# VectorE's order in the first product of a sparse feed-forward layer: an operation moved behind the second low part of w1, dot products regrouped

## The chip, the cores and the metric

The kernel runs on one NeuronCore of a Trainium2 chip (trn2). The metric is the device time of one execution in microseconds (us), as the median of several runs; lower is better.

## What is computed

A cross-attention layer is followed by a feed-forward layer in which each token uses only 56 of 3584 hidden rows. Both are residual. The change concerns the feed-forward layer alone:

```python
inter = xf @ c1_w.T @ c2_w.T                     # (1600, 3584), rank 16
blk = inter.reshape(B * T, n_blocks, SPARSITY)   # 56 blocks of 64
idx = jnp.argmax(blk, axis=-1) + jnp.arange(0, INTER, SPARSITY)
w1_g = w1[idx]
w2_g = w2t[idx]
h = jax.nn.relu(jnp.einsum('bkm,bm->bk', w1_g, xf))
out = jnp.einsum('bk,bkm->bm', h, w2_g)
```

There are 16 x 100 = 1600 tokens of 1024 features, all in float32. The attention ahead of it projects queries, keys and values, attends and projects back (`x1 = x + attention`).

## The kernel before

The stages follow each other, each in a block of its own with a barrier at its end: keys and values, queries, attention, the output projection, a normalisation, the gate's weights, then `hidden_layer` (the first product of the sparse layer, where the change is) and `project_down` (the second).

**Most tokens go the dense way.** For 1344 tokens `hidden_layer` computes the whole of `w1 @ x1t` and multiplies it by a mask of ones and zeros that holds the argmax. A float32 product is made of three products of high and low parts (`product`, 8 chunks x 3 = 24 matmuls of 128x336). w1 has 28 blocks of 128 rows, taken two at a time: 14 bodies (`i`), each of two halves (`p` = 0, 1), and block `j = 2i + p`. A half has four tiles of 336 tokens (`t` = 0 to 3), and so four calls of `sums(j, p, t)` on TensorE.

**256 tokens go the gathered way.** For them GpSimd gathers the chosen rows of w1 from DRAM into a ring of four buffers (`hid_ring`), and VectorE takes the dot product of each with its token (`dot(k)`): six per body from the second body on, 78 in all. A gather is issued when the dot product four places before it is done (`dotted`).

What each engine does in one half, in program order:

- TensorE: `sums` 0; `turn_w` (four transposes, the first half of the next block of w1, into PSUM bank `turn` 0); `gates` (the gate values of four token tiles, or one); `sums` 1; `turn_w` for the second half, into `turn` bank 1; `sums` 2; then the wait `pe.wait_ge(low, 2 * j + 4)`, for both low parts of the next block; `turn_mask` (11 and 2 transposes of the mask, into the same two banks, which is why they must be free); `gates` again; `sums` 3. A `sums` of tile `t` waits for `evacuate` of tile `t` of the half before.
- ScalarE: `high_part` rounds each half of the transposed w1 into `hid_w` (L1749), and `mask_part` copies the transposed mask into `hid_mask_t` (L1758).
- VectorE, the engine whose order is changed: `low_part` 0 and 1 (what the rounding left over, L1779); `pick`, which finds the argmax of a group of gate values in five operations: max (L1793), equality with it (L1795), multiplication by keys (L1797), max (L1801) and the mask itself (L1803); `indices` (once a body, L1809); `evacuate` 0 to 3 (relu and mask from PSUM to `h`, L1827); the `dot`s (L1546); and once a body `clip` (L1551). `evacuate` 0 waits for the transposed mask.
- SyncE loads blocks of w1 and stores `h` to `h_scratch`, after `evacuate` 3 of each half.

The first body is a special case: its first half makes all masks of the first pair, its second half (`late`) makes an extra one, and it has no dot products. The last body makes no masks.

In the trace `hid_raw` and `c_raw` are the loaded blocks of w1 (and `c_raw` also `h`), `turn` is the PSUM tile of transposes, `hid_acc` the PSUM tile of the sums, `w_l_raw` and `w_w_raw` the operands of `project_down`.

Of the kernel before, what the change touches and what calls it, by code (L numbers as in the profile page):

```python
# [1557 lines left out]
def hidden_layer(nc, sem, w1, x1t, c2s, zs, h_dram, ident, ident_bf, sparsity, stored, sparse, spare):  # L1558
# [11 lines left out]
    per = 2 * P // sparsity  # L1570

    picks = [(a, min(4, tt - a)) for a in range(0, tt, 4)]
    NP = len(picks)
# [11 lines left out]
    with ExitStack() as mem:  # L1585
# [31 lines left out]
        @block.sync  # L1617
        def _(sp):
            def load(j, p):
                sp.dma_start(raw[p][:, :], w1_v[bass.ds(j, 1)].rearrange("a p n -> (a p) n")).then_inc(landed[p], 16)  # L1620

            def store(j, p):
                sp.wait_ge(h_out, tiles * (j + 2))
                sp.dma_start(h_dram[bass.ds(j, 1)].rearrange("a p n -> (a p) n"), h[p][:, :]).then_inc(stored[p], 16)

            load(0, 0)
            load(1, 1)
            with sp.Fori(0, pairs - 1) as i:
                for p in range(2):

                    sp.wait_ge(turned, 2 * (2 * i + p + 1))
                    load(2 * i + p + 2, p)
                    store(2 * i + p, p)
            store(blocks - 2, 0)
            store(blocks - 1, 1)
# [139 lines left out]
        @block.vector  # L1775
        def _(dve):
            def low_part(j, p, s):
                dve.wait_ge(high, 2 * j + s + 1)
                dve.tensor_tensor(w[p][:, 1, 4 * s:4 * s + 4, :], turn[:, s, :].rearrange("q (c n) -> q c n", c=4),  # L1779
                                  w[p][:, 0, 4 * s:4 * s + 4, :].bitcast(F32), ALU.subtract).then_inc(low, 1)  # L1780

            def spread(ap, g):
                return ap.rearrange("q (a c) -> q a c", c=1).to_broadcast([P, g, sparsity])

            def pick(i, m, k):

                a, n = picks[k]
                g = n * per
                at = slice(a * per, a * per + g)
                done = NP * i + k  # L1790
                values = gate[:, :, :].rearrange("q a (b c) -> q (a b) c", c=sparsity)[:, :g, :]
                dve.wait_ge(gated, done + 1)
                dve.tensor_reduce(top[:, at], values, AX.X, ALU.max).then_inc(step, 1)  # L1793
                dve.wait_ge(step, 3 * done + 1)
                dve.tensor_tensor(equal[:, at, :], values, spread(top[:, at], g), ALU.is_equal).then_inc(compared, 1)  # L1795
                dve.wait_ge(compared, done + 2)
                dve.tensor_tensor(equal[:, at, :], equal[:, at, :],  # L1797
                                  key_bf[:, :].rearrange("q (a c) -> q a c", a=1).to_broadcast([P, g, sparsity]),
                                  ALU.mult).then_inc(step, 1)
                dve.wait_ge(step, 3 * done + 2)  # L1800
                dve.tensor_reduce(lead[:, at], equal[:, at, :], AX.X, ALU.max).then_inc(step, 1)  # L1801
                dve.wait_ge(step, 3 * done + 3)
                dve.tensor_tensor(mask[m][:, at, :], equal[:, at, :], spread(lead[:, at], g),  # L1803
                                  ALU.is_equal).then_inc(masked, 1)

            def indices(i):

                at = slice(i * per, (i + 1) * per)
                dve.tensor_tensor(sparse.idx[:, :, at],  # L1809
                                  base[:, at].rearrange("q (a c) -> q a c", a=1).to_broadcast([P, sparse.S, per]),  # L1810
                                  lead[:, :sparse.S * per].rearrange("q (a c) -> q a c", a=sparse.S),
                                  ALU.subtract).then_inc(idx_made, 1)

            def dot(k):
                kind, s, g = sparse.hidden[k]
                dve.wait_ge(gathered[k % slots], 16 * (k // slots + 1))
                sparse.dot(dve, s, g, ring[k % slots]).then_inc(dotted, 1)

            def evacuate(i, p, t):
                j = 2 * i + p  # L1820
                dve.wait_ge(summed, tiles * (j + 1) + t + 1)
                if t == 0:
                    dve.wait_ge(mask_out, 2 * j + 4)

                    dve.wait_ge(stored[p], 16 * (i + 1))
                at = slice(t * width, (t + 1) * width)
                dve.scalar_tensor_tensor(out=h[p][:, at], in0=acc[:, t, :width], scalar=0.0, in1=mask_t[:, at],  # L1827
                                         op0=ALU.max, op1=ALU.mult).then_inc(h_out, 1)

            def body(i, m, more, first):  # L1830
                for p in range(2):
                    j = 2 * i + p
                    early = first and p == 0
                    late = first and p == 1
                    dots = [] if first else [sparse.PER_PAIR * (i - 1) + sparse.PER_PAIR // 2 * p + n
                                             for n in range(sparse.PER_PAIR // 2)]
                    if early:
                        for k in range(NP):
                            pick(0, 0, k)
                            if k == 0:  # L1840
                                indices(0)
                    if late:
                        pick(1, 1 - m, 1)
                    if more or p == 0:
                        low_part(j + 1, 1 - p, 0)
                    if more and not early:
                        pick(i + 1, 1 - m, 2 * p)
                        if p == 0:
                            indices(i + 1)
                    if more or p == 0:  # L1850
                        low_part(j + 1, 1 - p, 1)
                    evacuate(i, p, 0)
                    for k in dots[:1]:
                        dot(k)
                    evacuate(i, p, 1)
                    if more:
                        pick(i + 1, 1 - m, 0 if early else 2 * p + 1)
                        if early:
                            indices(i + 1)
                    for k in dots[1:2]:  # L1860
                        dot(k)
                    evacuate(i, p, 2)
                    for k in dots[2:]:
                        dot(k)
                    evacuate(i, p, 3)
                if not first:
                    dve.wait_ge(dotted, sparse.PER_PAIR * i)
                    sparse.clip(dve, range(sparse.PER_PAIR * (i - 1), sparse.PER_PAIR * i)).then_inc(clipped, 1)

            dve.wait_ge(made, 2)  # L1870
            dve.wait_ge(base_made, 1)
            low_part(0, 0, 0)
            low_part(0, 0, 1)
            for i in range(pairs):
                body(i, i % 2, i + 1 < pairs, i == 0)
# [550 lines left out]
```

## Time and profile before

| | before |
|---|---|
| median of 3 runs | 3725.41 us (3724.01 to 3728.13) |
| the profiled execution | 3725.45 us, of which the span is 3723.7 us |
| granted TensorE clock, mean of the span | 0.973 of full speed |
| TensorE busy | 3479.5 us, 93% of the span |
| VectorE busy | 2323.2 us, 62% |
| ScalarE, GpSimd busy | 1415.3 us, 38%; 837.3 us, 22% |

The span is the time between the first and the last instruction that the profiler recorded; the execution's own time is 1.75 us longer. The granted clock is told as a share of 2.4 GHz. Busy shares are averages over all stages; what a change in one stage is worth has to be read from that stage, which here lasts from 2669 to 3208 us of the span.

### The profile page before, as it was taken

Reading aid. Unit: us, or ns where it says so; the run is one execution under the profiler, and the core shown is the slowest. Engines: PE = TensorE matmul, PEld = TensorE weight load, DVE = VectorE, ACT = ScalarE, POOL = GpSimd, SP = SyncE. Lnnn points to the kernel's source line nnn. Section 1 sums busy time; section 2 is a strip of 40 time slices with the busy share of each in tenths; the row PEclk is TensorE's granted clock in tenths of the full one; section 3 lists DMA queues with packets and bytes.
Section 4 is the critical chain, followed back from the end, with each engine's and each line's share of the span. In section 5 each row is a group of like instructions: output and inputs, shape, how many; then the busy total and the mean of one; then the engine's idle time right before and its main releaser. Section 6 shows DMA issues by size and latency. Waiting matters only on the chain. (4 is left out here: it accounts for less than half of the span.)

```text
span 3723.7 us, 52261 instructions
## 1 busy us (share of the span) xinstructions
PE 3479.5 (93%) x18370; PEld 3066.9 (82%) x18370; DVE 2323.2 (62%) x3935; ACT 1415.3 (38%) x2648; POOL 837.3 (22%) x1100
## 2 busy tenths in 40 slices
PE   6999999899999999999998999999799999699899
PEld 5888888799998888888887787787689999677676
DVE  5555575877665777777775333332578888566765
ACT  4333343444333777777775222221411111221321
POOL 0000000000002667666662100000011111233231
PEclk8999999899999999999999999999899999899999
DMA  3333333454444333333334545543334443698986
GB/s 124 100 105 97 99 98 90 115 134 115 121 121 124 103 108 90 105 104 108 105 86 145 144 118 154 154 119 93 110 116 150 143 154 137 254 287 277 302 285 199
DMA packets 525094, 520.73 MB, mean 140 GB/s; under 512 B 177668, under 2 KB 413188, under 8 KB 524884
## 3 DMA queue, kind: packets, MB, share of 16 engines
q1 hardware_dynamic: 489220, 391.06, 35.5%
q0 software_dynamic: 34608, 124.90, 10.1%
q8 instruction: 117, 1.92, 0.2%
q10 hardware_dynamic: 1056, 2.10, 0.2%
q14 instruction: 93, 0.76, 0.1%
HBM read 402.95 MB, written 115.02 MB: 139 GB/s over the span
## 5 line engine op out<-in xcount | busy, mean ns | idle before, releaser
L2083 PE MATMUL wo_acc<-wo_w,wo_l 128*128 128x512 f32 (+1 forms) x2496 | 573.7, 392 | 21.9 <-DVE wo_l L2033 21.8
L427 PE MATMUL kv_bank<-kv_wo,kv_so 128*128 128x512 f32 x2436 | 575.7, 396 | 15.8 <-DVE kv_wo L519 10.6
L2083 PEld LDWEIGHTS wo_acc<-wo_w,wo_l 128*128 128x128 f32 (+1 forms) x2496 | 460.2, 185 | 135.2 <-DVE wo_w L2057 24.7
L427 PEld LDWEIGHTS kv_bank<-kv_wo,kv_so 128*128 128x128 f32 x2436 | 458.7, 190 | 110.6 <-issue 16.7
L815 PE MATMUL pr_bank<-pr_xo,pr_wp 128*128 128x400 f32 x2688 | 500.6, 348 | 27.5 <-ACT pr_s L882 11.9
L815 PEld LDWEIGHTS pr_bank<-pr_xo,pr_wp 128*128 128x128 f32 x2688 | 495.4, 191 | 30.4 <-DVE pr_wp L899 22.6
L2312 PE MATMUL w_acc<-w_w,w_l 128*128 128x512 f32 (+1 forms) x1848 | 451.5, 404 | 60.9 <-DVE w_l L2287 60.0
L2312 PEld LDWEIGHTS w_acc<-w_w,w_l 128*128 128x128 f32 (+1 forms) x1848 | 344.8, 189 | 167.3 <-DVE w_l L2287 36.9
L26 PE MATMUL hid_acc<-x1t,hid_w 128*128 128x336 f32 x2688 | 442.6, 323 | 1.4 <-DVE c_raw L1827 0.9
L26 PEld LDWEIGHTS hid_acc<-x1t,hid_w 128*128 128x128 f32 x2688 | 426.4, 194 | 2.1 <-issue 1.1
L1311 PE MATMUL outs<-pt,v 128*128 128x384 f32 (+3 forms) x1536 | 347.3, 348 | 27.9 <-issue 14.0
L1409 DVE TENSOR_TENSOR pt<-turned,pt 128x512 fp32r<-128x512 f32 x384 | 264.1, 688 | 155.6 <-ACT pt L1361 152.6
L2033 DVE TENSOR_TENSOR wo_l<-wo_l_raw,wo_l 128x512 fp32r<-128x512 f32 (+1 forms) x208 | 139.4, 672 | 335.2 <-ACT wo_l L2006 335.1
L26 PE MATMUL scores<-kt,q_parts 128*128 128x462 f32 x1152 | 337.8, 402 | 1.2 <-ACT probs L1367 1.2
L1311 PEld LDWEIGHTS outs<-pt,v 128*128 128x128 f32 (+1 forms) x1536 | 277.4, 188 | 66.2 <-issue 30.4
L1239 POOL TENSOR_SCALAR probs<-probs,inverse 128x461 f32<-128x461 f32 x400 | 261.6, 654 | 249.9 <-DVE inverse L1405 249.7
L1361 ACT ACTIVATE pt<-turned 128x512 fp32r<-128x512 f32 x384 | 229.3, 597 | 168.5 <-PE turned L1292 165.2
L2006 ACT ACTIVATE wo_l<-wo_l_raw 128x512 fp32r<-128x512 f32 (+1 forms) x208 | 127.6, 615 | 397.7 <-PE wo_acc L2083 378.3
L1367 ACT ACTIVATE probs<-scores,negmax 128x461 f32<-128x461 f32 x400 | 257.6, 644 | 35.6 <-DVE negmax L1398 34.3
L1398 DVE TENSOR_REDUCE negmax<-scores 128x1 f32<-128x461 f32 x400 | 251.2, 628 | 23.8 <-PE scores L1276 23.2
L1292 PE MATMUL turned<-ident,probs 128*128 128x128 f32 x1600 | 240.7, 273 | 1.2 <-POOL probs L1239 1.2
L2244 ACT ACTIVATE w_l<-w_l_raw 128x512 fp32r<-128x512 f32 (+1 forms) x154 | 93.9, 611 | 335.5 <-DMA w_l_raw<-h_scratch 269.7
(185 smaller groups left out, 4182.3 us busy)
## 6 DMA issues: line engine op xcount, KB each, us to landing
wo_l_raw<-o_scratch SPq DMA_DIRECT2D x192, 256.0 KB, 2.9
w_l_raw<-h_scratch SPq DMA_DIRECT2D x140, 256.0 KB, 4.6
pair_raw<-in_L_xattn_Wq_dram SPq DMA_DIRECT2D x64, 512.0 KB, 5.6
q_scratch<-pr_out SPq DMA_DIRECT2D x128, 200.0 KB, 2.4
o_scratch<-o_stage SPq DMA_DIRECT2D x64, 400.0 KB, 3.5
q_raw<-q_scratch SPq DMA_DIRECT2D x64, 384.0 KB, 3.2
stage<-in_ctx_dram SPq DMA_DIRECT2D x45, 512.0 KB, 3.9
h_scratch<-c_raw SPq DMA_DIRECT2D x28, 672.0 KB, 5.5
```

The lines of the kernel that those rows point to most:

```text
L26: last = pe.matmul(out, left(a, c), right(b, c), start=(c == 0 and (a, b) == PAIRS[0]), stop=(c == chunks - 1 and (a, b) == PAIRS[-1]))
L427: last = pe.matmul(bank[:, BANK[i], :], so[:, i, a, c, :], wo[:, i, e, c, :], start=(not opened and c == 0 and (a, e) == PAIRS[0]), stop=( ...
L815: last = pe.matmul(bank[:, BANK[i], :width], wo[:, i, a, c, :], xo[:, i, e, c, :], start=(not opened and c == 0 and (a, e) == PAIRS[0]), s ...
L1239: pool.tensor_scalar(probs[:, I % RB, :kv], probs[:, I % RB, :kv], inverse[:, I % RB:I % RB + 1], 1.0, ALU.mult, ALU.mult).then_inc(scaled, 1)
L1292: last = pe.transpose(turned[:n, j % TB, k, :], probs[:, j % RB, at:at + n], ident[:, :])
L1311: last = pe.matmul(outs[:, h, :hi - lo], v[b % 2][:n, a, k, g * P:(g + 1) * P], pt[:n, e, k, lo:hi], start=(x == 0), stop=(x == NC * len(P ...
L1361: act.activation(pt_of(j, 0), turned[:, j % TB, :, :], ACT.Copy).then_inc(pt_high, 1)
L1367: act.activation(probs[:, I % RB, :kv], scores[:, I % SB, :kv], ACT.Exp, bias=negmax[:, I % RB:I % RB + 1], accum_out=total[:, I % RB:I % ...
L1398: dve.tensor_reduce(negmax[:, I % RB:I % RB + 1], scores[:, I % SB, :kv], AX.X, ALU.max, negate=True).then_inc(s_max, 1)
L1409: dve.tensor_tensor(pt_of(j, 1), turned[:, j % TB, :, :], pt_of(j, 0).bitcast(F32), ALU.subtract).then_inc(pt_low, 1)
L2083: last = pe.matmul(acc[p][:rows, :], l[j % 2][:, a, k, :rows], w[:, c, m * per + k, :], start=(m == 0 and k == 0 and (a, c) == PAIRS[0]), ...
L2312: last = pe.matmul(acc[n % 2][:heights[t], :], l[u % 2][:, a, k, :heights[t]], w[:, c, m * per + k, :], start=(m == 0 and k == 0 and (a, c ...
```

## The change

The mask operation is split off from `pick` into a function of its own, `mark`. In a half of a steady body the second `low_part` now stands between the two, so that it comes ahead of the mask operation. The dot products of a body, three in each half before, are now two in the first half and four in the second; the first two of a half stand in front of `evacuate` 0, where before only single ones stood between the evacuations. `evacuate` 0, 1 and 2 now follow each other, and the second `pick` of a half comes behind `evacuate` 2. No operation is added or taken away.

```diff
                 dve.tensor_reduce(lead[:, at], equal[:, at, :], AX.X, ALU.max).then_inc(step, 1)
+
+            def mark(i, m, k):
+
+                a, n = picks[k]
+                g = n * per
+                at = slice(a * per, a * per + g)
+                done = NP * i + k
                 dve.wait_ge(step, 3 * done + 3)
                 dve.tensor_tensor(mask[m][:, at, :], equal[:, at, :], spread(lead[:, at], g),
                                   ALU.is_equal).then_inc(masked, 1)
...
-                    dots = [] if first else [sparse.PER_PAIR * (i - 1) + sparse.PER_PAIR // 2 * p + n
-                                             for n in range(sparse.PER_PAIR // 2)]
+                    at = sparse.PER_PAIR * (i - 1)
+                    dots = [] if first else list(range(at, at + 2) if p == 0 else range(at + 2, at + sparse.PER_PAIR))
                     if early:
                         for k in range(NP):
                             pick(0, 0, k)
+                            mark(0, 0, k)
                             if k == 0:
                                 indices(0)
                     if late:
                         pick(1, 1 - m, 1)
+                        mark(1, 1 - m, 1)
                     if more or p == 0:
                         low_part(j + 1, 1 - p, 0)
                     if more and not early:
                         pick(i + 1, 1 - m, 2 * p)
+                    if more or p == 0:
+                        low_part(j + 1, 1 - p, 1)
+                    if more and not early:
+                        mark(i + 1, 1 - m, 2 * p)
                         if p == 0:
                             indices(i + 1)
-                    if more or p == 0:
-                        low_part(j + 1, 1 - p, 1)
+                    for k in dots[:2]:
+                        dot(k)
                     evacuate(i, p, 0)
-                    for k in dots[:1]:
-                        dot(k)
                     evacuate(i, p, 1)
+                    evacuate(i, p, 2)
                     if more:
                         pick(i + 1, 1 - m, 0 if early else 2 * p + 1)
+                        mark(i + 1, 1 - m, 0 if early else 2 * p + 1)
                         if early:
                             indices(i + 1)
-                    for k in dots[1:2]:
-                        dot(k)
-                    evacuate(i, p, 2)
                     for k in dots[2:]:
                         dot(k)
                     evacuate(i, p, 3)
```

What stands in VectorE's program, in a steady body, from `evacuate` 0 of the first half to the first low part of the second half (`hid_w0`), in the kernel before. The instruction with L1546 is a dot product; the one after it, which writes `value` alone, reads its sum out.

```order
L1827 SCALAR_TENSOR_TENSOR c2_raw<-hid_acc,hid_mask_t 128x336 [waits h_stored0,mask_out,h_summed]
L1546 ISA hid_ring0,value<-hid_ring0,keep0 128x1024 [waits row_gathered0]
L1546 ISA value 128x1
L1827 SCALAR_TENSOR_TENSOR c2_raw<-hid_acc,hid_mask_t 128x336 [waits h_summed]
L1793 TENSOR_REDUCE hid_top<-gate 128x16 [waits gated]
...
L1803 TENSOR_TENSOR hid_mask0<-hid_equal,hid_lead 128x1024 [waits mask_step]
L1546 ISA hid_ring1,value<-hid_ring1,keep1 128x1024 [waits row_gathered1]
L1546 ISA value 128x1
L1827 SCALAR_TENSOR_TENSOR c2_raw<-hid_acc,hid_mask_t 128x336 [waits h_summed]
L1546 ISA hid_ring2,value<-hid_ring2,keep0 128x1024 [waits row_gathered2]
L1546 ISA value 128x1
L1827 SCALAR_TENSOR_TENSOR c2_raw<-hid_acc,hid_mask_t 128x336 [waits h_summed]
L1779 TENSOR_TENSOR hid_w0<-turn,hid_w0 128x512 [waits w1_high]
```

The same place in the changed kernel, from two dot products on:

```order
L1546 ISA hid_ring0,value<-hid_ring0,keep0 128x1024 [waits row_gathered0]
L1546 ISA value 128x1
L1546 ISA hid_ring1,value<-hid_ring1,keep1 128x1024 [waits row_gathered1]
L1546 ISA value 128x1
L1834 SCALAR_TENSOR_TENSOR c2_raw<-hid_acc,hid_mask_t 128x336 [waits h_stored0,mask_out,h_summed]
L1834 SCALAR_TENSOR_TENSOR c2_raw<-hid_acc,hid_mask_t 128x336 [waits h_summed] x2
L1793 TENSOR_REDUCE hid_top<-gate 128x16 [waits gated]
...
L1810 TENSOR_TENSOR hid_mask0<-hid_equal,hid_lead 128x1024 [waits mask_step]
L1834 SCALAR_TENSOR_TENSOR c2_raw<-hid_acc,hid_mask_t 128x336 [waits h_summed]
L1779 TENSOR_TENSOR hid_w0<-turn,hid_w0 128x512 [waits w1_high]
```

Between the wait for the mask and the low part `hid_w0` there were three dot products; now there is none. One of them has gone to the second half, two stand ahead of the wait.

The second place is the start of the second half of a body on VectorE. Before:

```order
L1779 TENSOR_TENSOR hid_w0<-turn,hid_w0 128x512 [waits w1_high]
L1793 TENSOR_REDUCE hid_top<-gate 128x16 [waits gated]
L1795 TENSOR_TENSOR hid_equal<-gate,hid_top 128x1024 [waits mask_step]
L1797 TENSOR_TENSOR hid_equal<-hid_equal,hid_key_bf 128x1024 [waits compared]
L1801 TENSOR_REDUCE hid_lead<-hid_equal 128x16 [waits mask_step]
L1803 TENSOR_TENSOR hid_mask0<-hid_equal,hid_lead 128x1024 [waits mask_step]
L1779 TENSOR_TENSOR hid_w0<-turn,hid_w0 128x512 [waits w1_high]
L1827 SCALAR_TENSOR_TENSOR c2_raw<-hid_acc,hid_mask_t 128x336 [waits h_stored1,mask_out,h_summed]
```

Now, with the same five rows ahead of them:

```order
L1801 TENSOR_REDUCE hid_lead<-hid_equal 128x16 [waits mask_step]
L1779 TENSOR_TENSOR hid_w0<-turn,hid_w0 128x512 [waits w1_high]
L1810 TENSOR_TENSOR hid_mask0<-hid_equal,hid_lead 128x1024 [waits mask_step]
L1546 ISA hid_ring2,value<-hid_ring2,keep0 128x1024 [waits row_gathered2]
L1546 ISA value 128x1
L1546 ISA hid_ring3,value<-hid_ring3,keep1 128x1024 [waits row_gathered3]
L1546 ISA value 128x1
L1834 SCALAR_TENSOR_TENSOR c2_raw<-hid_acc,hid_mask_t 128x336 [waits h_stored1,mask_out,h_summed]
```

The second low part has moved ahead of one mask operation, and two dot products stand between the mask operation and `evacuate` 0.

## Rows read from the trace of the kernel before

**Rows 1.** The page: TensorE's and VectorE's busy time.

```profile
PE 3479.5 (93%) x18370; PEld 3066.9 (82%) x18370; DVE 2323.2 (62%) x3935; ACT 1415.3 (38%) x2648; POOL 837.3 (22%) x1100
```

**Rows 2.** Waits, 2669 to 3212 us: total us, times, longest.

```profile
DVE c_raw L1827 <- issue: 73.2, 27, 10.5
...
PE turn L1691 <- DVE hid_w L1779: 30.8, 14, 3.9
```

**Rows 3.** Timeline of TensorE, one body: start, us, what, count, [idle before <- releaser].

```profile
3144.41 3.93 PE L26 MATMUL hid_acc<-x1t,hid_w 128*128 128x336 f32 x24
3148.19 0.87 PE L1691 MATMUL turn<-ident_bf,hid_mask 128*128 128x128 bf16 x11
...
3149.56 7.60 PE L26 MATMUL hid_acc<-x1t,hid_w 128*128 128x336 f32 x48
3157.00 0.60 PE L1668 MATMUL turn<-ident,c_raw 128*128 128x128 f32 x4
...
3161.60 0.60 PE L1668 MATMUL turn<-ident,c_raw 128*128 128x128 f32 x4
3161.96 3.94 PE L26 MATMUL hid_acc<-x1t,hid_w 128*128 128x336 f32 x24
3167.99 0.86 PE L1691 MATMUL turn<-ident_bf,hid_mask 128*128 128x128 bf16 x11 [2.10 <-DVE hid_w L1779]
```

**Rows 4.** Timeline of VectorE, the same body.

```profile
3150.29 0.51 DVE L1827 SCALAR_TENSOR_TENSOR c_raw<-hid_acc,hid_mask_t 128x336 f32<-128x336 f32 x1 [2.57 <-issue]
3150.71 1.21 DVE L1546 CUSTOM_DVE_ANT_0 hid_ring<-hid_ring,keep 128x1024 f32<-128x1024 f32 x1
...
3151.85 0.50 DVE L1827 SCALAR_TENSOR_TENSOR c_raw<-hid_acc,hid_mask_t 128x336 f32<-128x336 f32 x1
3152.27 1.22 DVE L1793 TENSOR_REDUCE hid_top<-gate 128x16 f32<-128x1024 f32 x1
...
3156.76 1.22 DVE L1803 TENSOR_TENSOR hid_mask<-hid_equal,hid_lead 128x1024 bf16<-128x1024 bf16 x1
...
3161.02 0.68 DVE L1779 TENSOR_TENSOR hid_w<-turn,hid_w 128x512 fp32r<-128x512 f32 x1
3161.62 1.22 DVE L1793 TENSOR_REDUCE hid_top<-gate 128x16 f32<-128x1024 f32 x1
...
3166.11 1.22 DVE L1803 TENSOR_TENSOR hid_mask<-hid_equal,hid_lead 128x1024 bf16<-128x1024 bf16 x1
3167.25 0.68 DVE L1779 TENSOR_TENSOR hid_w<-turn,hid_w 128x512 fp32r<-128x512 f32 x1
```

**Rows 5.** Timeline of ScalarE, the same body: the first high part.

```profile
3157.63 0.60 ACT L1749 ACTIVATE hid_w<-turn 128x512 fp32r<-128x512 f32 x1 [7.43 <-PE turn L1668]
```

**Rows 6.** Timeline of TensorE: mask transposes of bodies 0, 1 and 5, second halves.

```profile
2714.22 1.41 PE L1691 MATMUL turn<-ident_bf,hid_mask 128*128 128x128 bf16 x11 [3.92 <-DVE hid_w L1779]
...
2753.89 0.90 PE L1691 MATMUL turn<-ident_bf,hid_mask 128*128 128x128 bf16 x11 [2.13 <-DVE hid_w L1779]
...
2904.77 1.41 PE L1691 MATMUL turn<-ident_bf,hid_mask 128*128 128x128 bf16 x11 [2.10 <-DVE hid_w L1779]
```

**Rows 7.** Stretches: length, busy us (PE, PEld, DVE, ACT, POOL), granted clock, DMA share, GB/s.

```profile
60.00:620.00 560.00, 560.00 (x2684) 467.85 (x2683) 321.53 (x562) 214.37 (x322) 6.61 (x8) 1.00 0.32 98
...
2904.77:2941.80 37.03, 36.33 (x243) 35.46 (x243) 30.06 (x45) 5.09 (x8) 6.93 (x6) 0.95 0.40 136
...
3131.00:3167.99 36.99, 34.89 (x243) 34.14 (x244) 31.40 (x46) 5.09 (x8) 6.93 (x6) 1.00 0.42 149
```

**Rows 8.** Timeline of the stage's last microseconds.

```profile
3202.49 0.51 DVE L1827 SCALAR_TENSOR_TENSOR c_raw<-hid_acc,hid_mask_t 128x336 f32<-128x336 f32 x1 [10.51 <-issue]
...
3207.17 0.50 DVE L1827 SCALAR_TENSOR_TENSOR c_raw<-hid_acc,hid_mask_t 128x336 f32<-128x336 f32 x1
...
3207.70 0.34 SPq L1624 DMA_DIRECT2D h_scratch<-c_raw  x1
```

**Rows 9.** The gathers' landing, 2740 to 3200 us.

```profile
DMA to landing us min/median/max: 3.8/6.5/9.0
```

## The prediction

> **What bounds the kernel now.** I read the page first: TensorE is busy 93% of the span, VectorE 62% [rows 1]. So VectorE can only matter where TensorE waits for it. The list of waits for the stretch of this stage shows one such place of size: the transposes of the mask waited 30.8 us in 14 waits for a low part of w1, the longest 3.9 us [rows 2]. The other direction is in the same list: `evacuate` stood idle 73.2 us in 27 times, put down to "issue" [rows 2]; its place in the program is behind the transposes and ScalarE's copy of the mask. So VectorE is late in one place and has idle time in another, once in each half.
>
> The two timelines of one body show where. TensorE starts the last `sums` ahead of the mask at 3144.41 and the mask's transposes at 3148.19, 3.78 us later, in the first half. In the second half it takes from 3161.96 to 3167.99, which is 6.03 us, with 2.10 us of idle time ahead of the transposes [rows 3]. The reader is to take the difference, 6.03 - 3.78 = 2.25 us, as the price of the wait, since it also holds the tail of a matmul whose end is only modelled. VectorE in that time [rows 4] starts the half's first low part at 3161.02, though ScalarE had the high part ready at 3157.63 + 0.60 = 3158.23 [rows 5]; it then runs five operations of `pick` and starts the second low part at 3167.25. It is 2.8 us late when the half begins.
>
> Third, the granted clock. The start of the mask's transposes in the second half repeats from 2714.22 (body 0) to 3167.99 (body 12) [rows 3, 6]: 12 periods in 453.77 us, 37.81 us each. A clean one is 36.99 us at a granted clock of 1.00 [rows 7]. The excess is 453.77 - 12 x 36.99 = 9.9 us. It comes in lumps: 2.7 us in the first period (2714.22 to 2753.89, 39.67 us), behind the longest wait, and 7.2 us in the other eleven. Where a lump begins, the eleven transposes behind the wait take 1.41 us in place of 0.86 [rows 3, 6], and the stretch that starts there has a clock of 0.95 [rows 7]: a short time at the lower of the two levels, 1.2 GHz, just behind a wait.
>
> **The change part by part.** No operation is added or removed, on any engine, and no DMA. All counts stay; only when things happen moves. I lay out the second half anew with the pitches (start to start) of the rows, and the first half's transposes at 3148.19 as before.
>
> *Dot products out of the way.* `evacuate` 0 starts at 3150.29, fixed by the mask [rows 4]. Then `evacuate` 1 and 2 at 0.42 us (3151.85 to 3152.27) each, so `pick` starts at 3151.13 + 0.42 = 3151.55; its first four operations take 4.49 us (3152.27 to 3156.76) and the mask operation 1.14 us (3166.11 to 3167.25): 3157.18; `evacuate` 3: 3157.60 [rows 4]. The first low part was at 3161.02 and could now start at 3157.60, but the high part is there only at 3158.23 [rows 5]. The three dot products that left this path gave 3 x 1.14 us (3150.71 to 3151.85) = 3.42 us, of which 2.79 us can be used.
>
> *Mask operation behind the low part.* From 3158.23: low part 0.60 us, four operations 4.49 us, so the second low part starts at 3163.32 (its high part is ready at 3161.60 + 0.63 + 0.60 = 3162.83) and ends 0.68 us later, at 3164.00 [rows 3 to 5]. TensorE would want it at 3161.96 + 3.78 = 3165.74 [rows 3]. It is 1.7 us early, and the whole 2.25 us of the wait go. Body 1 to 12: **12 x 2.25 = 27.0 us**.
>
> *What takes the dot products' place.* Behind the second low part come the mask operation (from 3163.92 to 3165.06) and two dot products. No row shows two in a row. Bounds: 1.14 us each, as ahead of an evacuation, or the full 1.22 + 0.08 us of operation and read-out, 1.30 us. They end at 3167.34 to 3167.66; the mask for `evacuate` 0 comes 2.10 us (3150.29 - 3148.19) behind the transposes, at 3167.84 [rows 3, 4]. They fit in idle time by 0.2 to 0.5 us, so they cost nothing; without that cover, `evacuate` 0 still has to be done only when TensorE starts `sums` 0, at 1.37 + 7.44 / 2 = 5.1 us behind the transposes (3148.19 to 3149.56, and half of 3149.56 to 3157.00), against 2.10 + 0.51 us [rows 3, 4]: 2.5 us to spare. The first half is alike. Its low part moved 1.14 us ahead where TensorE did not wait for it, worth nothing. SyncE's store follows `evacuate` 3, which in both halves comes no later than before; the next load of w1 behind it in the queue moves with it. GpSimd's gathers start when a dot product ends. The tightest pair of ring buffers is freed at 3167.3 and wanted by the next body's first half, whose `evacuate` 0 is at 3165.74 + 17.19 + 2.10 = 3185.03 (17.19 = 36.99 - 19.80, a clean body less 3148.19 to 3167.99 [rows 3, 7]), less two dot products: 15 us, against 9.0 us for the slowest landing [rows 9].
>
> A rule of the skill speaks against counting pitches like this. The evacuation's row says 0.50 us, but the next operation starts 0.42 us after it [rows 4]. The Trainium skill (VectorE: DVE Perf Modes, section "The DRAIN you can't avoid") holds that the next operation does not start until the pipe is empty, chained or not. By the rule three evacuations and two dot products cost 3 x 0.51 + 2 x 1.30 = 4.1 us instead of 3.5 us. The first low part would still be on time, and the sum would lose 0.5 us at the stage's tail.
>
> *The clock.* With no wait in front of them the lumps of bodies 2 to 12 should not start: **7.2 us**. The evidence is that a stretch of 560 us in which TensorE was never idle has a clock of 1.00 throughout [rows 7].
>
> *Body 0.* Its second half waits 3.92 us [rows 6]; only the mask operation moves there, 1.14 us. A shorter wait remains (2.8 us), between the 2.1 us of the others and 3.9 us. The lump of 2.7 us behind it is bounded by its whole size and by nothing; I take 0.6 us of it, since the wait that is left is longer than waits that were followed by one. **1.7 us**.
>
> *Tail.* In the last half the six operations from `evacuate` 0 (3202.49) to the start of `evacuate` 3 (3207.17) take 4.68 us [rows 8]; now one of three dot products stands ahead, so 3 x 0.42 + 2 x 1.14 (or 1.30) = 3.54 to 3.86 us. The store of `h` at 3207.70 follows directly and the next stage waits for it [rows 8]. **1.0 us**.
>
> **Sum.** 27.0 + 7.2 + 1.7 + 1.0 = 36.9 us. The profiled execution took 3725.45 us (span 3723.7 us), the median of three runs is 3725.41 us, so the two are the same here. 3725.4 - 36.9 = **3688.5 us**.
>
> **Rivals.**
> *The clock lumps stay* though the waits go, as something that comes with time and not with waits. For it: of twelve waits of about 2.1 us only some were followed by one. Against it: each begins at a wait, and none in the 560 us stretch. Then 27.0 + 1.1 + 1.0 = 29.1 us: 3696.3 us. Chance 0.10.
> *A shorter wait takes its place*, for instance for a low part that is still late because evacuations and dot products overlap less than I assume, or because TensorE, never stopping, wants it earlier. The margin of 1.7 us speaks against it. If 1 us per body stays, with half the lumps, 12 + 3.6 us are lost: 3704 us. Chance 0.05.
> *Only the mask operation's place matters*: the first low part does not start earlier, because something else than dot products holds it. Then 13 x 1.14 + 1.0 = 15.8 us: 3709.6 us. The idle-free row of VectorE up to 3161.02 [rows 4] speaks against it. Chance 0.03.
> *Slower: gathered rows come late.* Dot products now stand ahead of `evacuate` 0, which TensorE's next `sums` waits for, and in VectorE's queue everything else stands behind them, low parts too. If rows took longer than 15 + 2.5 us, every further microsecond would stop TensorE. To end 0.2% above before, it must eat 36.9 + 7.5 = 44.4 us in 12 bodies, 3.7 us each: rows that take 21 us from their buffer's release, against 9.0 us at most from issue [rows 9]. At 22 us it gives 3725.4 + 10 = 3736 us. Chance 0.03.
>
> **How the numbers follow.** My forecast holds 0.79. The time is that of the likeliest case. Its own bounds are 3686 (all of body 0's lump, full tail) to 3691 us (neither, and the drain rule); a few us more because runs of one kernel spread, the three shown by 4 us. With the clock rival inside, the range is 3685 to 3697 us and leaves out about 0.12. About 0.2% (7.5 us) is what a measurement of this kernel can tell from no change. All cases but the last are faster by more: 0.95; some 0.02 for a gain that is used up elsewhere; slower 0.03.
>
> **What the profile of the changed kernel would show.** The wait of the mask's transposes for a low part falls from 30.8 us in 14 waits to about 4.5 us in 2, both in body 0 (30.8 - 12 x 2.10 - 1.14). The mask's transposes of second halves repeat at 34.7 us (36.99 - 2.25). The granted clock is 1.00 in every body from the third on. The first low part of a second half has idle time of about 0.6 us ahead, put down to ScalarE, and the second none. Two dot products in a row are 1.14 to 1.30 us apart, which settles the drain rule. `evacuate` keeps an idle time, now under 1 us. The prediction is wrong if TensorE's list of waits shows a new one (for `hid_acc`, or for the gate's equality), if VectorE waits for gathered rows, or if lumps of clock stay in bodies that have no wait.

## The result and the profile after

The changed kernel takes 3689.74 us (median of four runs, 3684.86 to 3693.77) against 3724.71 us (four runs, 3720.31 to 3728.13) for the kernel before: a ratio of 0.9906, with a 95% interval of 0.9889 to 0.9923. That is 35.0 us less, where 36.9 us were forecast; 3689.74 us stands against a predicted 3688.5 us. The profiled execution took 3689.50 us, with a span of 3687.8 us.

The page's busy times and the list of waits of the changed kernel, from 2669 to 3175 us; a wait row has the total in us, the number of times and the longest.

```profile
PE 3460.4 (94%) x18370; PEld 3052.4 (83%) x18370; DVE 2321.1 (63%) x3935; ACT 1415.4 (38%) x2648; POOL 829.7 (22%) x1100
```

```profile
DVE hid_w L1779 <- ACT hid_w L1749: 38.4, 27, 6.1
DVE c_raw L1834 <- issue: 26.2, 28, 10.2
...
PE turn L1691 <- DVE hid_w L1779: 4.3, 2, 2.7
...
PE hid_acc L26 <- DVE c_raw L1834: 0.9, 1, 0.9
```

VectorE does the same work as before in 2321 us (2323 us in [rows 1]). What has changed is where its idle time lies. TensorE's wait for the low part has gone from 30.8 us in 14 waits [rows 2] to 4.3 us in 2. VectorE now waits more for ScalarE's high parts (38.4 us in 27 times, 23.2 us in 15 before), and less for the mask (26.2 us against 73.2 us).

Timeline of TensorE in one steady body of the changed kernel:

```profile
3013.81 0.87 PE L1691 MATMUL turn<-ident_bf,hid_mask 128*128 128x128 bf16 x11
...
3027.58 3.93 PE L26 MATMUL hid_acc<-x1t,hid_w 128*128 128x336 f32 x24
3031.35 0.87 PE L1691 MATMUL turn<-ident_bf,hid_mask 128*128 128x128 bf16 x11
...
3066.09 0.87 PE L1691 MATMUL turn<-ident_bf,hid_mask 128*128 128x128 bf16 x11
```

From the start of the last sums ahead of the mask to the start of its transposes it is now 3031.35 - 3027.58 = 3.77 us, as long as in the first half; in the kernel before it was 6.03 us in this place [rows 3]. A body lasts 3066.09 - 3031.35 = 34.74 us. Timeline of VectorE in the same body:

```profile
3013.12 1.22 DVE L1546 CUSTOM_DVE_ANT_0 hid_ring<-hid_ring,keep 128x1024 f32<-128x1024 f32 x1
3014.26 0.08 DVE L1546 DVE_READ_ACCUMULATOR2_ANT value<- 128x1 f32 x1
3014.26 1.22 DVE L1546 CUSTOM_DVE_ANT_0 hid_ring<-hid_ring,keep 128x1024 f32<-128x1024 f32 x1
3015.41 0.08 DVE L1546 DVE_READ_ACCUMULATOR2_ANT value<- 128x1 f32 x1
3015.91 1.34 DVE L1834 SCALAR_TENSOR_TENSOR c_raw<-hid_acc,hid_mask_t 128x336 f32<-128x336 f32 x3 [0.42 <-issue]
3017.16 1.22 DVE L1793 TENSOR_REDUCE hid_top<-gate 128x16 f32<-128x1024 f32 x1
...
3023.88 0.69 DVE L1779 TENSOR_TENSOR hid_w<-turn,hid_w 128x512 fp32r<-128x512 f32 x1 [0.59 <-ACT hid_w L1749]
...
3028.86 0.68 DVE L1779 TENSOR_TENSOR hid_w<-turn,hid_w 128x512 fp32r<-128x512 f32 x1
3029.45 1.22 DVE L1810 TENSOR_TENSOR hid_mask<-hid_equal,hid_lead 128x1024 bf16<-128x1024 bf16 x1
```

The first low part of the second half starts 3023.88 - 3013.81 = 10.07 us behind the first half's transposes, held by ScalarE and no longer by dot products; before it was 12.83 us (3161.02 - 3148.19 [rows 3, 4]). The second starts at 15.05 us and ends 1.8 us before TensorE wants it. The two dot products of a half end 0.4 to 0.5 us before the mask is there. Three evacuations go from 3015.91 to 3017.16 in pitch, 0.42 us each, and a dot product follows another after 1.14 us.

The stretches of the changed kernel: length, busy us of PE, PEld, DVE, ACT, POOL, granted clock, DMA share, GB/s.

```profile
2717.31:2753.49 36.18, 36.18 (x244) 35.56 (x244) 28.48 (x39) 5.09 (x8) 2.11 (x2) 0.95 0.29 97
2753.49:2788.23 34.74, 34.74 (x246) 34.15 (x244) 31.30 (x47) 5.09 (x8) 6.34 (x6) 1.00 0.47 161
...
2822.97:3135.55 312.58, 312.58 (x2188) 307.25 (x2188) 281.57 (x415) 45.83 (x72) 57.02 (x54) 1.00 0.46 161
```

From 2753.49 to 3135.55 us, from the mask's transposes in the second half of body 1 to those of body 12, TensorE is busy all the time and its clock is at 2.4 GHz throughout. Behind the second half of body 0 one lump of lower clock is left, behind the wait of 2.66 us: 36.18 - 34.74 = 1.4 us.

For the experiments I use a length that the rest of the kernel does not touch, called the stretch below: from the first transposes of the mask in the stage to the start of the last evacuation. The timelines have its start in the kernel before,

```profile
2692.12 0.86 PE L1691 MATMUL turn<-ident_bf,hid_mask 128*128 128x128 bf16 x11 [1.64 <-DVE hid_w L1779]
```

and, in the changed kernel, its start, the gates product and the first sums of body 0's second half behind it, and its end:

```profile
2696.50 0.86 PE L1691 MATMUL turn<-ident_bf,hid_mask 128*128 128x128 bf16 x11 [1.63 <-DVE hid_w L1779]
2697.29 1.10 PE L1679 MATMUL gate<-c2s,zs 80*128 80x256 f32 x4
2699.25 6.20 PE L26 MATMUL hid_acc<-x1t,hid_w 128*128 128x336 f32 x24 [0.86 <-DVE c_raw L1834]
```

```profile
3173.59 0.50 DVE L1834 SCALAR_TENSOR_TENSOR c_raw<-hid_acc,hid_mask_t 128x336 f32<-128x336 f32 x1
```

It was 3207.17 [rows 8] - 2692.12 = 515.05 us before and is 3173.59 - 2696.50 = 477.09 us now, 37.96 us less. Outside it the two profiled executions differ in stages that the change does not touch: the stretch started 4.38 us later and what follows it took 2.37 us less, which gives 35.95 us, the difference of the two executions (3725.45 - 3689.50). In the traces of all kernels here the program ahead of this point is the same, and the stretch starts anywhere between 2690.82 and 2698.82 us.

### The profile page after: what moved, and what is told of

Its sections match the earlier page's. It is cut to its first block and busy times, and to the rows that moved or that the text cites. A ratio compares the mean times of both kernels' runs of the same rounds, so it can differ in the third digit from the quotient of the medians.

```text
span 3687.8 us, 52261 instructions
## 1 busy us (share of the span) xinstructions
PE 3460.4 (94%) x18370; PEld 3052.4 (83%) x18370; DVE 2321.1 (63%) x3935; ACT 1415.4 (38%) x2648; POOL 829.7 (22%) x1100
```

## The experiments

All are built on the changed kernel and were run beside the kernel before. Four ran on one chip (kernel before 3721.76 us) and four on another (3728.55 us), neither time beside the runs of the result, so kernels of different occasions are compared by their ratios and by their stretches.

**Only the mask operation moved.** Dot products and evacuations stand as before.

```diff
-                    at = sparse.PER_PAIR * (i - 1)
-                    dots = [] if first else list(range(at, at + 2) if p == 0 else range(at + 2, at + sparse.PER_PAIR))
+                    dots = [] if first else [sparse.PER_PAIR * (i - 1) + sparse.PER_PAIR // 2 * p + n
+                                             for n in range(sparse.PER_PAIR // 2)]
...
-                    for k in dots[:2]:
-                        dot(k)
                     evacuate(i, p, 0)
+                    for k in dots[:1]:
+                        dot(k)
                     evacuate(i, p, 1)
-                    evacuate(i, p, 2)
                     if more:
                         pick(i + 1, 1 - m, 0 if early else 2 * p + 1)
                         mark(i + 1, 1 - m, 0 if early else 2 * p + 1)
...
+                    for k in dots[1:2]:
+                        dot(k)
+                    evacuate(i, p, 2)
```

Expected: 

> Only the mask operation is moved behind the second low part; dot products and evacuations stand as in the kernel before. Path theory (TensorE's wait is the time by which the second low part is late, and each operation moved off the way to it counts with its pitch): the wait of bodies 1 to 12 falls from 2.25 us by 1.14 us to 1.1 us each (about 0.96 us in the trace's idle column), that of body 0 from 3.9 to 2.7 us. The stage gets shorter by 13 x 1.14 = 14.8 us, and by up to 9.9 us more if the shorter waits are no longer followed by lumps of lower clock: 3700 to 3710 us. Rival (the mask operation's place alone made the gain): no wait in bodies 1 to 12, 3690 to 3692 us. Rival (lumps of lower clock come with time, not with waits): as the path theory, with about as many lumps as before, so at 3709 us whatever the waits are.

Measured: 3699.09 us, ratio 0.9936 (0.9922 to 0.9949). That is 0.9 us under the expected range, on a chip where the kernel before took 3.0 us less than in the result. The list of waits of this kernel, 2660 to 3212 us, and its stretches:

```profile
PE turn L1691 <- DVE hid_w L1779: 14.3, 14, 2.7
```

```profile
2714.86:2752.04 37.18, 36.34 (x244) 35.57 (x244) 27.78 (x40) 5.09 (x8) 3.46 (x3) 0.95 0.26 83
2752.04:3143.00 390.96, 382.61 (x2667) 374.64 (x2668) 341.24 (x504) 56.02 (x88) 76.16 (x66) 1.00 0.44 155
```

Of the 14.3 us, 4.3 us are the two waits of body 0, as in the changed kernel, so 10 us are left for twelve bodies: 0.8 us each in the idle column. A body is 35.73 us (3109.31 - 2752.04 over ten), 1.0 us above 34.74 us where 1.1 us was expected. Behind these short waits the clock stayed at 1.00. So, made alone, the mask's move is worth 36.99 - 35.73 = 1.26 us in each of twelve bodies, 15 us, beside it the 7.2 us of lumps in these bodies, and the same 2.5 us in body 0 as in the changed kernel. The stretch is 3184.20 - 2693.99 = 490.21 us, 24.8 us less than before. The path theory holds, and the rival that the mask operation's place alone made the gain falls: this kernel keeps a wait in each body, which costs 1.0 us. The rival on the clock expected 3709 us, with as many lumps as before, and falls too.

**Only the dot products regrouped.** The mask operation stands ahead of the second low part, as before.

```diff
-                    if more or p == 0:
-                        low_part(j + 1, 1 - p, 1)
                     if more and not early:
                         mark(i + 1, 1 - m, 2 * p)
                         if p == 0:
                             indices(i + 1)
+                    if more or p == 0:
+                        low_part(j + 1, 1 - p, 1)
```

Expected: 

> Only the dot products and evacuations are regrouped; the mask operation stays ahead of the second low part. Path theory: the first low part starts when its high part is there, 2.8 us earlier than before; the second then starts 0.60 + 4.49 + 1.14 us later and ends 0.6 us before TensorE wants it. No wait in bodies 1 to 12 and no lumps there, body 0 as in the kernel before (wait 3.9 us and its lump, together 2.5 us more than in the changed kernel): 3692 us. Rival (both edits are needed, because the second low part is 1.1 us late without the mask's move): 12 x 1.1 us and some lumps more than the changed kernel, 3703 to 3712 us. Rival (dot products were in idle time anyway and their place is worth nothing): 3725 us.

Measured: 3686.26 us, ratio 0.9905 (0.9890 to 0.9921), which can't be told from the changed kernel by time. The waits:

```profile
PE turn L1691 <- DVE hid_w L1779: 5.6, 2, 3.9
```

There is no wait in bodies 1 to 12. In one of them VectorE's second low part starts at 3029.81 and so ends at 3030.49 us, 0.6 us before TensorE starts the mask's transposes at 3031.05 us. The stretch is 3173.28 - 2693.57 = 479.71 us, 2.6 us longer than in the changed kernel (expected: 2.5 us), all of it in body 0, whose wait is 3.9 us again. So in the steady bodies the regrouping alone takes away the whole wait; beside it, the mask's move only widens the margin there, and what it adds in the changed kernel is in body 0. The rival that both edits are needed falls.

**The work put back on the path.** In the second half of bodies 1 to 12 the mask operation and the two dot products stand ahead of the second low part.

```diff
+                    behind = p == 1 and more and not first
+                    if behind:
+                        mark(i + 1, 1 - m, 2 * p)
+                        for k in dots[:2]:
+                            dot(k)
                     if more or p == 0:
                         low_part(j + 1, 1 - p, 1)
-                    if more and not early:
+                    if more and not early and not behind:
...
-                    for k in dots[:2]:
+                    for k in [] if behind else dots[:2]:
```

Expected: 

> The changed kernel, but in the second half of bodies 1 to 12 the mask operation and the two dot products stand ahead of the second low part instead of behind it. VectorE does the same work in the same half, in another order. Path theory: the second low part starts 1.14 + 2 x 1.14 us later, uses up the margin of 1.7 us and is 1.7 us late: 12 x 1.7 = 20 us more than the changed kernel, and 0 to 9 us for lumps of lower clock that come back behind the waits: 3710 to 3719 us. Rival (what helped is that VectorE's load is spread better over the halves, not the place of single operations): 3690 us. Rival on the clock (lumps come with time): one lump as in the changed kernel, 3710 us.

Measured: 3716.98 us, ratio 0.9992 (0.9982 to 1.0002): nearly all of the gain is gone. The waits, TensorE's timeline around one wait that was followed by a lump, and two bodies, the first without and the second with one:

```profile
PE turn L1691 <- DVE hid_w L1779: 24.0, 14, 2.7
```

```profile
2791.83 0.86 PE L1691 MATMUL turn<-ident_bf,hid_mask 128*128 128x128 bf16 x11 [1.64 <-DVE hid_w L1779]
...
2792.84 9.08 PE L26 MATMUL hid_acc<-x1t,hid_w 128*128 128x336 f32 x48
...
2829.82 0.86 PE L1691 MATMUL turn<-ident_bf,hid_mask 128*128 128x128 bf16 x11 [1.64 <-DVE hid_w L1779]
...
2830.84 7.59 PE L26 MATMUL hid_acc<-x1t,hid_w 128*128 128x336 f32 x48
```

```profile
2755.30:2791.83 36.53, 34.89 (x244) 34.14 (x244) 31.38 (x46) 5.10 (x8) 6.34 (x7) 1.00 0.44 153
2791.83:2829.82 37.99, 36.35 (x244) 35.61 (x244) 31.38 (x46) 5.10 (x8) 6.33 (x7) 0.96 0.43 147
```

A body without a lump is 36.53 us, 1.79 us above the changed kernel's (expected: 1.7 us), with the same 31.4 us of VectorE's work in it. After some of the waits of 1.64 us the 48 matmuls that follow take 9.08 us instead of 7.59 us. The stretch is 3202.66 - 2696.53 = 506.13 us, 29.0 us longer than in the changed kernel: 12 x 1.79 = 21.5 us for the waits and 7.5 us, five lumps of 1.5 us, for the clock. How the load is spread over the halves is the same as in the changed kernel, so the rival that this made the gain falls. The rival on the clock falls too: it expected no lumps beyond that of the changed kernel. Why five of the twelve waits, all of 1.64 us, were followed by a lump and the others not stays open.

**Body 0 in another order.** Its second half has both low parts ahead of the second search, the evacuations behind it, and two mask operations behind these.

```diff
                     if late:
                         pick(1, 1 - m, 1)
-                        mark(1, 1 - m, 1)
+                        low_part(j + 1, 1 - p, 0)
+                        low_part(j + 1, 1 - p, 1)
+                        pick(i + 1, 1 - m, 2)
+                        evacuate(i, p, 0)
+                        evacuate(i, p, 1)
+                        evacuate(i, p, 2)
+                        mark(1, 1 - m, 1)
+                        mark(i + 1, 1 - m, 2)
+                        pick(i + 1, 1 - m, 3)
+                        mark(i + 1, 1 - m, 3)
+                        evacuate(i, p, 3)
+                        continue
```

Expected: 

> The changed kernel with another order in the second half of body 0 alone: both low parts stand ahead of the second search for the maximum, and two mask operations behind the evacuations. Path theory: both low parts are there when ScalarE has the high parts, some 2 us before TensorE wants them, so the wait of 2.66 us goes, and with it the lump of 1.4 us behind it: 4.1 us less than the changed kernel, 3685.6 us. Rival (the lump stays, since the clock is low early in the stage for another reason): 2.7 us less, 3687 us. Rival (evacuation 0, behind the search, is now late and stops the next sums of TensorE): a wait of hid_acc for evacuation takes the place, 0 to 2 us less or more.

Measured: 3682.63 us, ratio 0.9886 (0.9871 to 0.9901). TensorE in body 0 of this kernel:

```profile
2698.82 0.86 PE L1691 MATMUL turn<-ident_bf,hid_mask 128*128 128x128 bf16 x11 [1.64 <-DVE hid_w L1779]
2699.62 0.74 PE L1679 MATMUL gate<-c2s,zs 80*128 80x256 f32 x4
2701.57 3.93 PE L26 MATMUL hid_acc<-x1t,hid_w 128*128 128x336 f32 x24 [1.22 <-DVE c_raw L1834]
...
2710.91 0.71 PE L1679 MATMUL gate<-c2s,zs 80*128 80x256 f32 x4 [0.82 <-DVE hid_equal L1795]
...
2715.59 0.86 PE L1691 MATMUL turn<-ident_bf,hid_mask 128*128 128x128 bf16 x11
```

The wait ahead of the last row is gone and so is the lump behind it. The stretch is 3170.49 - 2698.82 = 471.67 us, 5.4 us less than in the changed kernel where 4.1 us was expected. The difference is the clock once more: the first sums of the second half took 3.93 us here, and 6.20 us at the lower clock in the changed kernel, while a gates product now waits 0.82 us for an equality that VectorE has not done. No evacuation became late. This part is not shown to be the edit's: the gates product ahead of these sums already took 0.74 us in place of 1.10 us, before TensorE reaches anything that the edit moved, and the same order of body 0 had 5.48 us for the same sums in the experiment "Body 0 and four dot products together". What the path theory named, the wait and the lump behind it, accounts for 2.8 + 1.4 = 4.2 us. What put the clock higher in those first sums was not tested.

The other four ran together, with the changed kernel itself beside the three others.

**The changed kernel again.** Expected: 

> The changed kernel once more, on the same chip and beside the same runs as the three kernels below. Every theory expects what was measured of it: about 3689 us, between 0.989 and 0.992 of the kernel before.

Measured: 3686.04 us, ratio 0.9886 (0.9870 to 0.9903). The stretch is 3173.88 - 2696.82 = 477.06 us, against 477.09 us: the stage repeats to some hundredths of a microsecond in these two traces, while whole executions spread by several, so differences of a few us are read from the stretch. It repeats only where the clock falls in the same places, as the two kernels with body 0 reordered show.

**Four dot products ahead of the first evacuation.**

```diff
-                    dots = [] if first else list(range(at, at + 2) if p == 0 else range(at + 2, at + sparse.PER_PAIR))
+                    dots = [] if first else list(range(at, at + 4) if p == 0 else range(at + 4, at + sparse.PER_PAIR))
...
-                    for k in dots[:2]:
+                    for k in dots:
                         dot(k)
...
-                    for k in dots[2:]:
-                        dot(k)
                     evacuate(i, p, 3)
```

Expected: 

> The changed kernel with four dot products ahead of evacuation 0 in the first half and two in the second, and none behind the second search. In the first half evacuation 0 then starts 2 x 1.14 - 0.5 = 1.8 us behind its mask, within the 2.5 us that TensorE's next sums leave it, and the first low part of the second half is 1.8 - 0.6 = 1.2 us behind its high part, within the margin of 1.7 us of the second low part. Path theory with margins: no new wait of TensorE, bodies of 34.7 us as in the changed kernel, and a tail shorter by 0.7 us: 3688 to 3689 us. Rival (whatever delays evacuation 0 costs TensorE its time): 12 x 1.8 us more, 3711 us. Rival (the margins are smaller than worked out): 0.1 to 1 us per body more, 3690 to 3701 us.

Measured: 3687.92 us, ratio 0.9886 (0.9868 to 0.9904). TensorE's waits, and VectorE's low parts in one body (the second half's transposes are 34.73 us apart here, 3028.95 to 3063.68 us):

```profile
PE turn L1691 <- DVE hid_w L1779: 4.3, 2, 2.7
...
PE hid_acc L26 <- DVE c_raw L1834: 0.9, 1, 0.9
```

```profile
3015.30 1.33 DVE L1834 SCALAR_TENSOR_TENSOR c_raw<-hid_acc,hid_mask_t 128x336 f32<-128x336 f32 x3
...
3022.59 0.68 DVE L1779 TENSOR_TENSOR hid_w<-turn,hid_w 128x512 fp32r<-128x512 f32 x1
...
3027.56 0.68 DVE L1779 TENSOR_TENSOR hid_w<-turn,hid_w 128x512 fp32r<-128x512 f32 x1
```

Evacuation 0 no longer has idle time ahead of it, nor has the first low part; both are late against what they wait for, and TensorE has no new wait. The stretch is 3170.38 - 2694.07 = 476.31 us, 0.75 us less than in the changed kernel (expected: 0.7 us). The margins that were worked out from the rows of before hold for this much lateness.

**Body 0 and four dot products together.** The two edits above, both.

Expected: 

> The order of body 0 from the earlier experiment together with four dot products ahead of evacuation 0 in the first halves. Path theory: the two add up, since they are in different bodies: 5.4 us and 0.7 us less than the changed kernel, 3683 to 3684 us, and in the trace no wait of TensorE for a low part but the one in the first half of body 0. Rival: the margins of the four dot products do not hold, 3685 to 3695 us.

Measured: 3678.95 us, ratio 0.9865 (0.9849 to 0.9881), the lowest median of all kernels here. The stretch is 3165.61 - 2694.34 = 471.27 us, 5.8 us less than in the changed kernel of the same occasion, where 5.4 + 0.7 = 6.1 us was expected. TensorE's only wait for a low part is the one in the first half of body 0, and the first sums behind it ran in part at the lower clock:

```profile
2697.09 5.48 PE L26 MATMUL hid_acc<-x1t,hid_w 128*128 128x336 f32 x24 [1.22 <-DVE c_raw L1834]
```

The two edits add up but for the clock in these sums. Its median is 7.1 us below that kernel's (3686.04 us); the runs of the two do not overlap (3675.2 to 3682.03 us against 3684.69 to 3687.45 us), and the trace accounts for 5.8 us of it.

**A ring of two buffers.** A row is fetched only when the dot product two places before it is done.

```diff
-    R_HIDDEN, R_DOWN, PER_PAIR = 4, 8, 6
+    R_HIDDEN, R_DOWN, PER_PAIR = 2, 8, 6
```

Expected: 

> The changed kernel with a ring of two buffers for gathered rows instead of four, so that a row is fetched only when the dot product two places before it is done. This takes the 15 us that a row has from its buffer's release down to about 5 us for the last two dot products of a body, less than the 6.5 us that a row takes at the median. Theory: VectorE waits some 2.5 to 4 us in each body for rows, the last evacuation and the next first low part come 1 to 2 us later, and the margins of the first half (0.6 us of idle time and 2.5 us of lead) take nearly all of it: 0 to 1 us per body of wait for TensorE, 3689 to 3702 us. Rival (late rows stop everything behind them one for one): 12 x 3 us and lumps of lower clock, 3725 us or more.

Measured: 3690.8 us, ratio 0.9902 (0.9885 to 0.9918). Its waits:

```profile
DVE hid_ring L1546 <- DMA hid_ring<-in_L_ffn_w_dram,idx: 18.5, 27, 1.2
...
PE turn L1691 <- DVE hid_w L1779: 4.3, 2, 2.7
```

VectorE now waits for rows, 18.5 us in all, 0.7 us a time, and TensorE does not notice: the stretch is 3167.87 - 2690.82 = 477.05 us, within 0.04 us that of the changed kernel in both of its profiles. The lateness was less than expected (1.5 us a body, not 2.5 to 4 us). Rows landed sooner than in the kernel before, 5.1 us behind their issue at the median against 6.5 us [rows 9]; so they did in the second trace of the changed kernel with its four buffers (5.1 us too), so it is not the ring that brought it. How much of the difference it explains was not tested. Rows that are late by up to 1.2 us do not reach TensorE. A row that is later than the margins was not made.

## Why the prediction was right

Each term against the trace of the changed kernel:

| term | predicted | measured |
|---|---|---|
| waits of bodies 1 to 12 | 27.0 us | 27.0 us, 12 x (36.99 - 34.74) |
| lumps behind them | 7.2 us | 7.2 us, clock 1.00 from 2753.49 us on, five lumps before |
| body 0: wait and part of its lump | 1.7 us | 1.3 + 1.2 = 2.5 us |
| tail | 1.0 us | 1.1 us, 4.68 us to 3.54 us |
| sum | 36.9 us | 37.8 us (the whole stretch: 37.96 us) |

- **The path.** First low part held by its high part with 0.6 us of idle time (measured 0.59 us), second low part 1.7 us early (1.8 us), dot products done 0.2 to 0.5 us ahead of the mask (idle time of 0.4 to 0.5 us). The two single-edit kernels and the one with the work put back show that the place of single operations ahead of the low part decided it, and not the load.
- **Which edit did it.** The prediction credited the two edits one after the other and so gave the mask's move more than it is worth beside the other. By its own numbers the first edit leaves the second low part 0.6 us early: 3158.23 + 0.60 + 4.49 + 1.14 + 0.68 = 3165.14 us against 3165.74 us. The experiment shows that beside the regrouping nothing in bodies 1 to 12 hangs on the mask's place; without it the same move saves 1.26 us a body.
- **The clock.** That lumps begin at waits was read from six of them. It is now shown both ways: no waits, no lumps; waits of 1.64 us put back, five lumps of 1.5 us back. The prediction says that the eleven transposes behind the wait take 1.41 us where a lump begins; that holds for three of the six, and the other three took 0.90 us (at 2753.89 us [rows 6]), 1.17 and 1.28 us and had their lump all the same. The term was mis-sized only in body 0, where I took 0.6 us of the lump and 1.2 us came.
- **The drain rule.** The Trainium skill (VectorE: DVE Perf Modes, "The DRAIN you can't avoid") holds that the next operation does not start until the pipe is empty, and by this the prediction gave three evacuations and two dot products 4.1 us. The same section adds that an operation that is not held back starts earlier, which the prediction left out. The rows agree with the addition. The five operations took 3.54 us at the stage's tail in the changed kernel, by the pitches of [rows 4]: the next operation starts 0.08 us before the one in front ends, and a dot product starts as the read-out of the one before it does.
- **The rivals.** The clock rival, the shorter wait and the mask-only rival each had a place where they would show in the trace, and none showed. Late rows did not occur; with the ring halved they occur, up to 1.2 us late, and cost TensorE nothing. For rows of 22 us the prediction's own terms give 12 x (22 - 17.5) - 36.9 = 17 us more than before, 3742 us and not the 3736 us that it says; nothing else in it is worked out from this figure.
- **What was off.** The whole execution gained 35.0 us at the median and the stage 38.0 us. The rest lies outside the stage, where executions differ by as much. So the terms came out 1 us above the forecast and the execution 2 us below it; that the time is met within 1.2 us is in part luck, since runs of this kernel spread by 9 us. The tail's 3.54 us was right, its wording was not: the last half has four dot products, two ahead of `evacuate` 0 and two in the tail, and not three with one ahead.

## What to carry to other kernels

When a strict queue feeds the bounding engine, write down for each operation when its input is ready and when its result is wanted, and put work without a deadline where the queue waits for something anyway; the same work costs 29 us or nothing by its place alone. Cost two edits of one path together and each alone, since the second may find nothing left to save. A wait of TensorE can cost more than its length, in the matmuls behind it, so the gain of a removed wait is read from the period of the loop and not from the idle column.

## What the runs showed of the hardware that was not expected

- Waits of 0.83 us in each of twelve bodies (1.0 us of the body's time) were followed by no fall of the clock, waits of 1.64 us by a fall in five of twelve, and waits of 2.1 us, in the kernel before, also in five of twelve (7.2 us at 1.44 us each). Each such fall cost 1.4 to 1.5 us, and so did the one behind the 2.7 us wait that the changed kernel has left; the waits of 3.9 us in body 0 were followed by 2.7 us.
- Two waits close together, 1.64 us and then 0.86 us within 3 us, at the turn from the first to the second half of body 0, were followed by a fall that cost 2.3 us: the first sums took 6.20 us in place of 3.93 us. In the two kernels with body 0 reordered the same sums, behind the same work of TensorE, took 3.93 and 5.48 us. So a wait's length alone does not settle whether the clock falls.
- A dot product of 128x1024 with its sum read out has a pitch of 1.14 us both ahead of an evacuation and ahead of another dot product, less than the 1.22 us that its own row gives. The prediction had left the second case between 1.14 and 1.30 us.
